# Clearing a masked quarter of the attention scores once per buffer instead of in every copy

## The reference

```
q, k, v = split(x @ qkv_w.T + qkv_b)                  # 16 heads of 8 channels
q, k = relu(q) + 1e-6, relu(k) + 1e-6
out[t] = sum over s <= t of (q[t].k[s]) v[s] / max(sum over s <= t of q[t].k[s], 1e-6)
x = layernorm(x + out @ out_w.T + out_b)              # first attention: causal, linear
x = layernorm(x + softmax window attention of x over ctx (|t-s| <= 64) @ proj.T + proj_b)
x = layernorm(x + top-1 mixture of 8 experts, 128 -> 512 -> 128, with a capacity)
```

## Time and profile before

| | us |
|---|---|
| median of 3 runs | 474.26 (473.88 to 474.88) |
| profiled execution | 473.45 |
| its span, first to last instruction | 471.7 |
| PE busy | 422.2 (89%) |
| PEld busy | 337.8 (72%) |
| DVE busy | 351.5 (75%) |
| ACT busy | 268.1 (57%) |
| POOL busy | 258.6 (55%) |

### The profile page before, as it was taken

One profiled execution on the slowest core, in us unless ns is written; L12 is line 12 of the kernel. 1 busy time (PEld: TensorE's weight loads), 2 busy tenths in 40 slices (PEclk: granted clock), 3 DMA queues, 4 the chain that ended last, 5 costly groups with the idle time before them and its releaser, 6 DMA issues.

```text
span 471.7 us, 20960 instructions
## 1 busy us (share of the span) xinstructions
PE 422.2 (89%) x7850; PEld 337.8 (72%) x7850; DVE 351.5 (75%) x1670; ACT 268.1 (57%) x655; POOL 258.6 (55%) x374
## 2 busy tenths in 40 slices
PE   8889999999999999999999999998746699999950
PEld 7666777778777778777777777776535478887740
DVE  4466667888888888888888898887673277778750
ACT  4456667667767667777667777666532333345400
POOL 5422355655666655666655666654552046757753
PEclk9999999999999999999999999999975799999995
DMA  4800000110110110110100100000014223334000
GB/s 137 266 15 15 14 25 15 31 33 25 29 35 26 33 31 27 30 32 26 37 27 27 34 18 20 20 17 13 19 35 118 85 84 103 103 108 134 25 17 20
DMA packets 25719, 22.50 MB, mean 48 GB/s; under 512 B 3606, under 2 KB 21072, under 8 KB 25620
## 3 DMA queue, kind: packets, MB, share of 16 engines
q1 hardware_dynamic: 23284, 16.96, 12.3%
q0 software_dynamic: 2336, 4.20, 2.8%
HBM read 12.13 MB, written 9.58 MB: 46 GB/s over the span
## 4 chain that ended last, share of the span: by engine, by line
PE 65%; ACT 17%; issue 9%; DVE 3%; POOL 2%; DMA 2%; POOLq 0%; ACTq 0%; DVEq 0%; SPq 0%
PE banks L567 24%; PE banks L623 13%; PE banks L810 8%; ACT arena L836 7%; PE banks L575 7%; ACT arena L936 6%; ACT arena L835 4%; PE banks L560 4%; PE banks L787 3%; PE banks L635 1%; DMA expert_in<-x,sidx 1%; PE banks L536 1%; PE banks L720 1%; PE banks L807 1%; DMA EB<-expert_in 1%
## 5 line engine op out<-in xcount | busy, mean ns | idle before, releaser
L1080 DVE TENSOR_REDUCE mx<-banks 128x8 f32<-128x1024 f32 x64 | 77.9, 1219 | 21.1 <-PE banks L575 21.1
L440 POOL TENSOR_TENSOR rs<-ve,minus_half 128x1 f32<-128x1 f32 x32 | 18.3, 570 | 105.1 <-DVE ve L1047 105.1
L865 ACT ACTIVATE arena<-banks 128x1024 f32<-128x1024 f32 x64 | 62.0, 1021 | 15.0 <-PE banks L575 15.0
L835 ACT ACTIVATE arena<-banks,first_half 128x512 f32<-128x512 f32 x64 | 44.1, 689 | 46.4 <-PE banks L575 46.4
L623 PE MATMUL banks<-arena,V 128*32 128x128 f32 x2048 | 69.4, 276 | 0.1
L936 ACT ACTIVATE arena<-banks,b1T 128x321 f32<-128x321 f32 x64 | 33.8, 529 | 55.1 <-PE banks L787 54.4
L623 PEld LDWEIGHTS banks<-arena,V 128*32 128x32 f32 x2048 | 51.9, 109 | 9.6 <-issue 5.3
L502 POOL DMA_INDIRECT out_x<-ot,idx x40 | 40.5, 1012 | 24.5 <-DVE ot L1277 15.8
L471 POOL DMA_INDIRECT expert_in<-x,sidx x32 | 35.5, 1109 | 11.5 <-DVE x L1153 4.8
L567 PE MATMUL banks<-x1T,CE 32*128 32x128 f32 x1024 | 37.5, 282 | 4.5 <-ACT arena L836 0.6
L567 PE MATMUL banks<-QE,kT 32*128 32x128 f32 x1024 | 37.7, 282 | 3.4 <-DVE mx L1080 1.3
(11 more groups left out here) (175 smaller groups left out, 1025.4 us busy)
## 6 DMA issues: line engine op xcount, KB each, us to landing
w_sb<-in_L_ffn_W SPq DMA_DIRECT2D x16, 256.0 KB, 3.1
expert_in<-zeros SPq DMA_DIRECT2D x10, 266.5 KB, 3.6
EB<-expert_in SPq DMA_DIRECT2D x8, 325.0 KB, 4.2
X<-in_x SPq DMA_DIRECT2D x32, 64.0 KB, 2.0
C<-in_ctx SPq DMA_DIRECT2D x32, 64.0 KB, 2.7
out_x<-fb SPq DMA_DIRECT2D x32, 64.0 KB, 1.5
out_x<-ot,idx POOLq DMA_INDIRECT x40, 2.2
b2b<-in_L_ffn_b SPq DMA_DIRECT2D x1, 512.0 KB
```

The lines of the kernel that those rows point to most:

```text
L835: nc.scalar.activation(to[:, :, :, 0:W2C], at_bank[:, :, :, 0:W2C], ACT.Relu, scale=first_half[:])
L865: nc.scalar.activation(P2[b % 2][:, 2 * half:2 * half + 2].rearrange("p j a t -> p j (a t)"), pair("s2t", half), ACT.Exp, scale=SCALE).the ...
L1080: v.tensor_reduce(mx[b % 2][:, 8 * half:8 * half + 8].rearrange("p (j a) -> p j a", a=NA), pair("s2", half).rearrange("p j (a t) -> p j a ...
```

## The change

The scores' ACTIVATE on the tokens 0..63 (line 835) keeps its form for blocks 0 and 1, which are the first users of the two buffers: it writes zeros to the partitions 64..127. For blocks 2 to 31 it is replaced by one that works on partitions 0..63 alone and has no scale operand. The zeros from blocks 0 and 1 stay in the buffers. Line 836 and everything else is as before.

```diff
             def op_s1e(b, half):
+
                 act.wait_ge(s1_full, b + 1)
                 wait(act, pv1_full, b - 1)
                 to = A1[b % 2][:, 2 * half:2 * half + 2]
                 at_bank = pair("s1", half).rearrange("p j (a t) -> p j a t", a=NA)
-                nc.scalar.activation(to[:, :, :, 0:W2C], at_bank[:, :, :, 0:W2C], ACT.Relu, scale=first_half[:])
+                if b < 2:
+                    nc.scalar.activation(to[:, :, :, 0:W2C], at_bank[:, :, :, 0:W2C], ACT.Relu, scale=first_half[:])
+                else:
+                    nc.scalar.activation(to[0:W2C, :, :, 0:W2C], at_bank[0:W2C, :, :, 0:W2C], ACT.Relu)
                 nc.scalar.activation(to[:, :, :, W2C:P], at_bank[:, :, :, W2C:P], ACT.Relu).then_inc(s1_out[half], 1)
```

## The result

The changed kernel took 470.43 us (median of 6 runs, 469.55 to 471.57) beside 474.91 us for the kernel before (473.88 to 475.82). The ratio is 0.9908, with a 95% interval of 0.9888 to 0.9928. By that ratio it takes 4.4 us less, between 3.4 and 5.3. The forecast was 471.0, 3.3 us less.

What follows compares the result with a forecast made beforehand. PE was taken as the bound, with only its standstill to win. Slack of 6.8 us less 3.45 us of handover gave 3.3 us, so 474.26 - 3.3 = 471.0 us; 8-in-10 range 468.6 to 473.6 us.

Steps and rivals of the forecast that it cites:

- ScalarE's saving: Scores' copies on ScalarE: two copies give back 0.10 and 0.09 us, so the last ends 0.19 us earlier each pass.
- Both far ends of that price: New copy on 64 partitions: bounds of 0.27 us from below and 1.02 us from above; 0.60 us was taken.
- What PE can take at s2t: Start of s2t after C's transpose on PE: it could move 0.15 to 0.19 us earlier each pass.
- pass 33: Pass with no scores to copy, used as reference: s2t starts 0.26 us after C's transpose starts.
- What is late next: PE's transpose of the first norm's block, waiting for GpSimd: only about 0.11 of 0.19 us gets past.
- The sum: Over 30 passes: 6.8 us of slack less 30 x 0.115 = 3.45 us of handover gives 3.3 us.
- Rival (a): GpSimd's result is no obstacle at the transpose; all of ScalarE's shortening passes: 5.7 us, 468.6 us; chance 0.12.
- (b): TensorE keeps its own issue gap before s2t and gains less: 0.6 to 2.4 us, 472.8 us; chance 0.12.
- (c): The new ScalarE copy takes 0.69 us like the old one: no change, 474.3 us; chance 0.13.
- The 0.09 us of issue: Time on PE before s2t's first matmul, after ScalarE's four copies, in the chain of waits.
- (d): DVE's small operations collide with GpSimd's: slower, 484.1 us; chance 0.07 together with a dear form of the copy.
- the new wait: Predicted in the list of waits: line 560, PE's transpose, waiting for GpSimd's line 446, some 30 times.

Runs made afterwards that it cites:

- The shorter root: Changed kernel with GpSimd's root of the first norm taken from the variance directly, without DVE's addition of 1e-5: 468.85 us, ratio 0.9881.
- the block on DVE behind oh: Changed kernel with the first norm's normalised block computed by DVE, not GpSimd, after the chosen-expert table: 478.24 us, 0.9964; once more 469.69 us, 0.9916.
- The third estimate, on the slower chip: Changed kernel unaltered, run again on a chip where the kernel before took 480.35 us: 476.92 us, ratio 0.9937.
- with ScalarE done 0.58 us ahead: Changed kernel without the copy of tokens 0..63 of the second half of the heads for blocks 2 to 31: 471.02 us, ratio 0.9914.
- the kernel before with the shorter root: Kernel before with only GpSimd's root of the first norm taken from the variance directly, 1e-5 left out: 475.38 us, ratio 1.0012.
- the block on DVE ahead of oh: Changed kernel with the first norm's normalised block computed by DVE right after q, before the chosen-expert table, not by GpSimd: 471.94 us, ratio 0.9948.

## Why the prediction was right

The mechanism was the forecast's, step by step, and the time fell in its range. That 470.43 lies only 0.6 us from the 471.0 is in part luck: the gain was 1.1 us larger than forecast by the ratio, and the kernel before, taken as 474.26 us from three runs, was 474.91 over six, which hides about 0.6 of it.

- ScalarE's saving: 0.19 us a pass forecast, 0.20 measured. The scale column is worth 0.09 us a copy (0.689 to 0.600, and 0.677 to 0.588), 0.18 a pass. The halved partitions, which no row of before could price, bring another 0.03 a pass, and bring it in the copy behind the halved one, where the forecast had nothing. Both far ends of that price, 0.27 and 1.02 us, were far off.
- What PE can take at s2t: 0.15 to 0.20 us forecast from pass 33, 0.20 measured. Forecast from this was a start 0.23 to 0.27 us after C's transpose; it is 0.21. The lower end of the saving came from the start of C's transpose, which in pass 33 is recorded 0.33 us long; the reading from its end, 0.07 us before, was exact.
- What is late next: the block's transpose, with a handover of 0.115 us. Measured 0.11 to 0.12 in all 30 passes, and the pass of 9.94 us was forecast to the hundredth. The shorter root and the block on DVE behind oh, which both end this wait in the usual pass and both bring it to 9.84 us, showed that it holds the pass.
- The sum: 3.3 us forecast; 3.64 us in the trace over the 29 passes. About 0.3 us of the difference is no gain of the change: one pass of before took 10.36 us for 10.05, and three more 10.09 to 10.12, against one of 10.09 in the changed kernel. The timed 4.4 and 3.8 us have intervals of some 1 us to either side, and 3.3 lies in the second and just outside the first. The third estimate, on the slower chip, is 3.0 us (1.5 to 4.5).
- Rival (a), 30 x 0.19 = 5.7 us, would have needed a pass of 9.86; (b) and (c) would have left a gap before s2t that is gone. The 0.09 us of issue on which (b) rested is the distance from the last copy's end to s2t, 0.10 us before and after; with ScalarE done 0.58 us ahead, s2t started only 0.01 us sooner after C's transpose. (d) did not come: line 1074, now 1078, takes 1.06 us in 18 of its 32 passes, where it took 1.00 to 1.06 in 24 before, and DVE still idles 0.21 us before mx in the pass shown.

Two things were read wrongly. The forecast said that the new wait would stand in the list of waits under GpSimd some 30 times. It does not; this is the list of the changed kernel (us in total, times, longest):

```profile
PEld banks L560 <- issue: 13.7, 67, 0.3
...
PE banks L560 <- POOL x L446: 0.9, 1, 0.9
```

A wait of 0.1 us behind other small matmuls is not attributed to anyone. It was found by the constant distance from its cause in the timeline, and by the experiments. And the forecast took the rest of the program as unchanged. In the profiled execution the span fell only 1.9 us, since the time from the thirtieth s2t to the end grew from 151.8 to 153.1 us and the first s2t came 0.4 us later. The granted clock in two windows, before and then changed, goes with it:

```profile
300.00:345.00 45.00, 38.25 (x863) 29.31 (x859) 35.18 (x193) 27.89 (x75) 23.66 (x33) 1.00 0.06 18
...
400.00:460.00 60.00, 54.09 (x383) 44.46 (x381) 44.41 (x188) 21.16 (x40) 39.46 (x42) 1.00 0.26 76
```

```profile
300.00:345.00 45.00, 37.49 (x776) 28.63 (x776) 34.71 (x187) 25.56 (x70) 23.42 (x32) 0.93 0.06 19
...
400.00:460.00 60.00, 52.22 (x366) 42.60 (x364) 43.02 (x181) 21.15 (x40) 39.38 (x41) 0.96 0.27 76
```

In the changed kernel the windows hold some time at 1.2 GHz that they did not before; the first of it comes from about 339 us on, behind 14 us in which PE was busy for 10.4 and waited for DVE and ScalarE. The other traces show that this differs from run to run: the changed kernel that ran beside the block on DVE behind oh has 0.99 and 1.00 in these windows, and the kernel before with the shorter root 0.93 and 1.00. So it is no effect of the change alone. The six timed runs of the changed kernel have mean clocks from 0.951 to 0.962, and the profiled one is the slowest of them.

## What to carry to other kernels

Where an engine is released by one wait and meets the next a microsecond later, read the slack of the second before you price the first: its distance from its cause less the shortest distance seen anywhere in the trace. Take that shortest distance where the consumer really waited. Here that gave 0.11 us out of 0.20 and the pass to the hundredth. Such a wait need not stand in the list of waits, so look for a distance that no longer varies. And the operand column that only cleared a quarter cost 0.09 us on each instruction: it is the column, not the partitions it masks, that was worth taking out.

## What the runs showed of the hardware

An ACTIVATE of 512 columns from PSUM took 0.600 us on 128 partitions and 0.588 on 64; with a scale column 0.689 and 0.677. The copy on 128 partitions that follows it got shorter too, 0.604 to 0.585 us, and 0.599 to 0.581 with the scale column. The starts of the copies lie as far apart with 64 partitions as with 128; only the scale column moved them, from 0.49 to 0.59 us for the first copy.

A late start of one matmul can delay what is behind it by more. With the block on DVE ahead of oh, rk's matmul starts 1.70 us after s2t at the median, 0.03 us behind its usual 1.67, but the load of the transpose behind it comes at 1.79, 0.08 us behind its usual 1.71, although its block had been ready for 0.38 us. No experiment asked why.
